# Weighting two of four edge tiles on GpSimd instead of VectorE, in a graph-attention aggregation

## The reference, cut to what matters

```
xl  = (x @ Wl).reshape(n, H, D)                    # H = 4 heads, D = 64, so 256 columns
p   = exp(e - m[dst])                              # one weight per edge and head
out = segment_sum(alpha[..., None] * xl[src], dst) # alpha = p / denom[dst]
```

## Time and profile before

| | us |
|---|---|
| median of 3 runs | 1134.26 |
| lowest and highest | 1133.28, 1134.72 |
| span of the profiled execution | 1132.4 |
| stage `aggregate`, from the barrier at 620.2 to that at 862.0 | 241.8 |
| busy in the span: PE | 993.6 (88%) |
| busy in the span: DVE | 909.5 (80%) |
| busy in the span: ACT | 615.7 (54%) |
| busy in the span: POOL | 391.9 (35%) |

### The profile page before, as it was taken

One profiled execution on the slowest core, in us unless ns is written; L12 is line 12 of the kernel. 1 busy time (PEld: TensorE's weight loads), 2 busy tenths in 40 slices (PEclk: granted clock), 3 DMA queues, 4 the chain that ended last, 5 costly groups with the idle time before them and its releaser, 6 DMA issues. The chain is left out here.

```text
span 1132.4 us, 16757 instructions
## 1 busy us (share of the span) xinstructions
PE 993.6 (88%) x5061; PEld 803.7 (71%) x5061; DVE 909.5 (80%) x1574; ACT 615.7 (54%) x1379; POOL 391.9 (35%) x398
## 2 busy tenths in 40 slices
PE   2697799999999999999956899999995797999964
PEld 1585789999999999999933777777774343454432
DVE  5875568888878888888886899999983768878886
ACT  3264456666666666666634677777773333334331
POOL 0212777777777777777300000000001100000000
PEclk9899989999999999999977899999997898999986
DMA  9354689889888989988534777899882433233222
GB/s 236 49 190 116 202 257 277 267 264 276 266 267 280 301 263 298 284 277 262 150 111 175 235 219 245 235 272 269 226 225 94 100 99 91 73 89 93 59 33 55
DMA packets 108048, 220.28 MB, mean 195 GB/s; under 512 B 24384, under 2 KB 56729, under 8 KB 107853
## 3 DMA queue, kind: packets, MB, share of 16 engines
q1 hardware_dynamic: 86537, 153.86, 42.1%
q0 software_dynamic: 19920, 55.84, 21.5%
q10 hardware_dynamic: 1508, 9.52, 2.5%
HBM read 157.22 MB, written 72.50 MB: 203 GB/s over the span
## 5 line engine op out<-in xcount | busy, mean ns | idle before, releaser
L985 POOL DMA_INDIRECT score_gath<-xl_rows,misc x324 | 342.0, 1056 | 103.2 <-issue 95.5
L1025 PE MATMUL score_ps_m<-x_hi,score_w_hi 128*128 128x416 f32 (+1 forms) x576 | 209.7, 364 | 1.8 <-DVE score_w_lo L1178 1.7
L1026 PE MATMUL score_ps_m<-x_lo,score_w_hi 128*128 128x416 f32 (+1 forms) x576 | 204.8, 356 | 0.0
L1027 PE MATMUL score_ps_m<-x_hi,score_w_lo 128*128 128x416 f32 (+1 forms) x576 | 204.2, 354 | 0.0
L1622 PE MATMUL ps_all<-agg_gath,agg_hot 128*125 128x256 f32 x648 | 184.9, 421 | 16.2 <-DVE agg_hot L1723 15.7
L1674 ACT ACTIVATE agg_gath<-agg_gath,prob 128x64 f32<-128x64 f32 x648 | 158.6, 338 | 6.8 <-DMA agg_gath<-edge_rows 6.4
L1157 DVE TENSOR_TENSOR score_zb<-score_gath,score_ps_x 128x1024 f32<-128x1024 f32 x81 | 98.8, 1220 | 76.8 <-PE score_ps_x L1008 67.2
L1622 PEld LDWEIGHTS ps_all<-agg_gath,agg_hot 128*125 128x125 f32 x648 | 99.6, 190 | 50.1 <-issue 42.5
L1624 PE MATMUL ps_all<-ext,agg_hot 128*125 128x18 f32 x324 | 118.3, 365 | 0.0
L1025 PEld LDWEIGHTS score_ps_m<-x_hi,score_w_hi 128*128 128x128 f32 x576 | 110.0, 191 | 3.8 <-issue 2.0
L1026 PEld LDWEIGHTS score_ps_m<-x_lo,score_w_hi 128*128 128x128 f32 x576 | 110.1, 191 | 1.1
(11 more groups left out here) (324 smaller groups left out, 1694.7 us busy)
## 6 DMA issues: line engine op xcount, KB each, us to landing
edge_rows<-score_gath SPq DMA_DIRECT2D x81, 520.0 KB, 4.0
agg_gath<-edge_rows SPq DMA_DIRECT2D x81, 520.0 KB, 4.7
local_bc<-local_rows SPq DMA_DIRECT2D x40, 224.0 KB
score_gath<-xl_rows,misc POOLq DMA_INDIRECT x324
xb_rows<-in_x ACTq DMA_DIRECT2D x1, 5000.0 KB, 17.4
phi_c<-phi_rows SPq DMA_DIRECT2D x10, 500.0 KB, 3.9
xb_rows<-in_L_mix_bo POOLq DMA_DIRECT2D x10, 500.0 KB, 6.9
x_bo<-xb_rows SPq DMA_DIRECT2D x10, 500.0 KB
```

Of the source, the lines that this page charges most:

```text
L985: nc.gpsimd.indirect_dma_start(out=gath[:, g % GS, q, :], out_offset=None, in_=xl_rows, in_offset=bass.IndirectOffsetOnAxis(ap=src_idx[:, ...
L1025: pe.matmul(acc, w_hi[:, i % 2, kk, :], x_hi[:, kk, cols], start=(kk == 0), stop=False)
L1026: pe.matmul(acc, w_hi[:, i % 2, kk, :], x_lo[:, kk, cols], start=False, stop=False)
L1027: mm = pe.matmul(acc, w_lo[:, i % 2, kk, :], x_hi[:, kk, cols], start=False, stop=(kk == KC - 1))
```

## The change

DVE no longer runs `weigh`; POOL runs the same instruction on the same data. POOL weighs groups 0 and 1, then adds the first bias, and then goes through the groups; the DMAs of piece p come behind the weighting of the group that lies four behind the end of that piece. PE's waits, ACT's share and the buffers are as before.

```
             @block.gpsimd
             def _(pool):
-                pool.wait_ge(k.s_xb, 16)
-                add_bias(nc, a, k, 0)
-                for p, (c, half) in enumerate(PIECES):
+                def weigh(g):
+                    pool.wait_ge(s_load[g % GS], 16 * (g // GS + 1))
+                    rows = gath[:, g % GS, 0:DQ, 0:HID].rearrange("p q (h d) -> p q h d", h=HEADS)
+                    nc.gpsimd.tensor_tensor(rows, rows, k.prob[:, g * GP:g * GP + DQ, :].unsqueeze(3).to_broadcast([P, DQ, HEADS, DH]),
+                                    ALU.mult).then_inc(s_weigh, 1)
+
+                def add_piece(p):
+                    c, half = PIECES[p]
                     pool.wait_ge(s_piece, p + 1)
                     if half == 0:
                         pool.wait_ge(k.s_xbo, 16 * (c + 1))
                         add_bias(nc, a, k, c + 1)
                     nc.gpsimd.dma_start(k.xb_rows[C * c:C * c + C, half * 512:(half + 1) * 512], piece[:, :], accum_op=ALU.add
                                         ).then_inc(k.s_part, 16)
+
+                weigh(0)
+                weigh(1)
+                pool.wait_ge(k.s_xb, 16)
+                add_bias(nc, a, k, 0)
+                for g in range(2, NG + 5):
+                    if g < NG:
+                        weigh(g)
+                    for p in range(len(PIECES)):
+                        if g == ENDS_AT[p] + 4:
+                            add_piece(p)
...
             @block.vector
-                def weigh(g):
-                    v.wait_ge(s_load[g % GS], 16 * (g // GS + 1))
-                    rows = gath[:, g % GS, 0:DQ, 0:HID].rearrange("p q (h d) -> p q h d", h=HEADS)
-                    v.tensor_tensor(rows, rows, k.prob[:, g * GP:g * GP + DQ, :].unsqueeze(3).to_broadcast([P, DQ, HEADS, DH]),
-                                    ALU.mult).then_inc(s_weigh, 1)
-
...
                 for g in range(NG):
-                    weigh(g)
                     one_hot(g)
```

## The result

The changed kernel takes 1139.85 us (median of 4; 1138.89 to 1142.74) where the kernel before takes 1133.84 (median of 4 runs): a ratio of 1.0050 with a 95% interval of [1.0033, 1.0067], so 6 us slower. The forecast was 1139.5.

The account below looks back on a forecast made before the run. DVE was taken to bound `aggregate`. Span 1132.4 + 10.2 (holds, less the removal) + 2 (start) - 7.1 (`finish`) = 1137.5; with the median 1.9 above the span 1139.4, written 1139.5 us; range 1121 to 1155.

Parts of the forecast that it names:

- DVE bounds, PE is next: In `aggregate`, DVE sets the period of six groups at 17.99 us; PE would need 16.7 us.
- first rival: "PE becomes the bound": in `aggregate`, DVE held under 2.4 us a period, so PE's 16.7 rules: 1121 us, chance 0.18.
- What is removed: In `aggregate`, 81 weighings leave DVE, 0.61 us each, 3.66 us a period, so its own work falls to 14.33.
- The multiply's length: In `aggregate`, POOL's 512-wide multiply takes 1.14 to 1.22 us, twice the 256-wide one in `finish`.
- The holds: In `aggregate`, POOL's multiplies block DVE about 1.0 us per meeting, 4.5 us a period, making 18.8: +10.2 us.
- The start: At the head of `aggregate`, POOL's library load delays group 0 to 629.2 or 632.1; DVE loses 2 us, bounds 0 to 3.
- The end: In `finish`, POOL's library is already loaded, so 7.1 us fall out of the chain.
- Moved DMAs at no cost: In `aggregate`, the bias and piece DMAs issued behind later weighings add nothing, covered by about 15 us of slack.
- Tensor_scalars are not held: In `aggregate`, 1024-number tensor_scalars escape the hold, so holds total 3.5 us a period: 1127 up to 1132 us, chance 0.12.
- POOL is slower: In `aggregate`, POOL's multiply takes 1.48 us, a period of 21.0: 1165 us, halfway 1152, chance 0.10.
- The load does not move: In `finish`, POOL still reloads its library, so the 7.1 us stay: 1146.6 us, chance 0.05.
- POOL held by DVE: By the skill's rule POOL also stands while a DVE instruction runs; no row showed it, and the sum stays unchanged.

Follow-up runs that it names:

- e3: The kernel before without DVE's weighing, tiles 0 and 1 summed unweighted, PE waiting for the load instead: 1117.46 us, ratio 0.9844.
- e5: The kernel before plus a tiny early POOL multiply in `maxima`; POOL weighs one group of six, beside DVE's reduction: ratio 0.9889.
- e1: The kernel before plus one tiny POOL multiply behind the reduction in `maxima`: 1130.24 us against 1135.71, ratio 0.9952.
- e4: The changed kernel with POOL's multiply replaced by a memset of the same rows: 1116.02 us, ratio 0.9830 to the kernel before.
- e9: The kernel before, DVE still weighing, plus the changed kernel's POOL stream multiplying a spare tile nobody waits for: ratio 1.0375.
- e6: The kernel before plus a tiny early POOL multiply; POOL weighs one group of six, beside DVE's tensor_scalars: ratio 0.9966.
- e2: The changed kernel plus a tiny POOL multiply behind the reduction in `maxima`: 1139.46 us, ratio 1.0045 to the kernel before.
- e7: The changed kernel as it is, run on another chip: ratio 1.0046 to the kernel before on that chip.

## Why the prediction was right, by its steps

- **DVE bounds, PE is next.** Right in order. The size of PE's period was off: 16.7 was inferred from 15.7 us of waits, PE's starts in e3 show 16.26. The view of waits did not hold all the time that PE lost to DVE: for the same nine periods PE's records are 150.91 us long in the kernel before (679.68 to 841.59) and 146.36 in e3, so some 0.5 us of a period stood inside PE's busy time. So the first rival would have been lower than 1121, and the room between DVE and PE was 1.7 us of a period, not 1.3.
- **What is removed, 3.66 us a period.** e3 confirms it: 17.99 - 14.38 = 3.61. e5 has 0.57 for its one weighing.
- **The multiply's length, 1.14 to 1.22.** It is 1.04 unheld (e5), below the range: one 256-wide multiply has more fixed time than the spacing of two showed.
- **The holds, 4.5 us a period.** Measured 18.92 - 14.33 = 4.6. The mechanism is right, but that the size is met so closely is in part luck, since errors cancelled: most holds are 0.62 to 0.73 for short instructions and 0.79 to 0.85 for long ones, not 1.0, and they come 69 times in 81, four of them much longer (last section), where 4.5 whole holds in six would be 61. The 0.14 us that DVE can do beforehand carried over as it was (L1475 ends 712.43, POOL 711.88, so 0.13 of its 0.69 was done). What was missing is that POOL's multiply has already run for a while when the DVE instruction that it holds starts: in that meeting from 710.83 to 711.02, so 1.05 - 0.19 - 0.13 = 0.73 is left as the hold. DVE's ending 0.28 us behind POOL, as in `finish`, holds for the add of 0.42 us alone; L1475 ends 0.56 behind, L1467 1.07.
- **The start, +2.** The first period is 3.9 us longer than 17.99; of that 0.9 is what every period now costs, 3.0 is the start. PE began its first group at 630.98, inside 629 to 632, but the loss was of another kind, and that +2 came near it is luck: DVE did not wait for PE there, it was held for 4.5 us behind a DMA and through a burst.
- **The end, -7.1.** Measured -7.0. e1 and e4 show it to be the wait before POOL's first arithmetic behind the reduction.
- **Moved DMAs at no cost.** e4 bears it out for the DMAs as such. In the changed kernel, though, the four longest holds begin while POOL issues one of them (last section), a meeting that the prediction did not count.
- **Which rival was alive.** "PE becomes the bound" falls by e9: an unused multiply costs the same. "Tensor_scalars are not held" falls by the row at 711.02 and by e6. "POOL is slower" falls by the 1.04 us of an unheld multiply. "The load does not move" falls by the configuration at 620.6 and the 0.10 us where 7.13 stood.
- **POOL held by DVE**, for which no row stood before, is what e6 shows: POOL waits 0.32 us for DVE's tensor_scalar, then DVE 0.72 for POOL. That agrees with the rule of the Trainium skill (SBUF — State Buffer, "Who interferes with whom") that whoever issues first keeps the port pair for the whole instruction. It did not move the sum, since POOL had time.

The sum was 1137.5 for the span and it was 1141.0; +3.5 is 2.6 in the stage (14.8 against 12.2), 0.1 in `finish`, and 0.9 outside of what was touched. The median, 1139.85, comes closer to 1139.5 than the steps do, which is luck.

## What to carry to other kernels

Moving an elementwise instruction from VectorE to GpSimd need not free VectorE of its time: here 0.61 us were saved and 0.73 paid, as a mean over the 81. Find meetings of the two engines elsewhere in the same trace, read how much longer VectorE's record is there than where the same instruction runs alone, and charge that for each meeting, scaled to the length of GpSimd's instruction. What can be moved is what fits beside a VectorE instruction that is not held, and it must be made to start there (e5). One input is no sign of that: the reduction was not held, the tensor_scalars were, even by a memset (e4). And look for an idle GpSimd just before its first arithmetic behind a reduction over partitions: one tiny instruction early takes it away.

## What the runs showed of the hardware that was not expected

A few holds are several times longer than the others. In the changed kernel POOL, then DVE:

```profile
632.12 1.07 POOL L58 DMA_DIRECT2D xb_rows<-in_L_mix_bo  x1
632.91 4.34 POOL L1594 TENSOR_TENSOR agg_gath<-agg_gath,prob 128x512 f32<-128x512 f32 x4
```

```profile
632.63 5.18 DVE L1474 TENSOR_SCALAR agg_work<-agg_work 128x1024 int32<-128x1024 int32 x1
637.85 0.69 DVE L1475 TENSOR_SCALAR agg_work<-agg_work 128x1024 f32<-128x1024 f32 x1
```

An instruction of 0.69 us took 5.18, through four multiplies whose inputs were all ready; DVE, which by its record had started first, got no turn between them. Once more, at 774.22, L1489 took 4.38 us through two multiplies:

```profile
774.22 4.38 DVE L1489 TENSOR_TENSOR agg_xq<-agg_work,agg_small 128x1024 bf16<-128x1024 f32 x1
```

```profile
774.27 1.17 POOL L1603 DMA_DIRECT2D xb_rows<-agg_piece  x1
774.82 2.69 POOL L1594 TENSOR_TENSOR agg_gath<-agg_gath,prob 128x512 f32<-128x512 f32 x2
```

That multiplies follow each other is not enough for this. In the first burst of e2, two multiplies in a row from 620.47, DVE did get its turn between them: L1727 ends at 621.53 and L1728 starts at 621.57. What the long holds have in common is a DMA that POOL issues just before. In the changed kernel four of the 69 holds are over 1.0 us (4.49, 3.16, 1.87 and 1.28), and each begins while POOL issues a DMA, with a multiply behind it; the same is so of every hold over 1.0 us in e2, e7 and e9. In e4 the hold of 2.84 us begins at 623.12 behind a DMA issued at 622.92 too, with memsets in place of multiplies. With nothing behind it such an issue holds nobody: in the kernel before no DVE instruction of the stage is lengthened by 0.1 us. No run took the DMA or the burst away alone, so which of the two decides, and why, stays open. An estimate of what it costs: the four meet eight multiplies; at the usual 0.73 each they would be 5.8 us together and are 10.8, so some 5 of DVE's 59 us.
